# A gated delta-rule layer: from two steps in flight to three, with a new order on every engine

## The chip, the cores and the metric

The kernel runs on one core of one Trainium2 chip. The metric is device time in microseconds, from one launch; lower is better. The engines are TensorE (PE; its weight loads PEld), VectorE (DVE), ScalarE (ACT), GpSimd (POOL) and SyncE (SP), which only issues DMAs. Each runs its own instruction list in order and waits on counting semaphores.

## The reference, cut to what matters

x is 8 x 1024 x 128, float32. The time goes to the attention layer; a small FFN (layer norms, three 128x128 matmuls) follows.

```python
q = silu(causal_conv4(x @ Wq.T)); k = silu(causal_conv4(x @ Wk.T))   # 16 heads of 64
v = silu(causal_conv4(x @ Wv.T))                                     # 16 heads of 128
q, k = q/|q|, k/|k|
alpha = exp(-exp(A_log) * softplus(x @ Wa.T + dt_bias)); beta = 2*sigmoid(x @ Wb.T)
# per batch and head, over t:
S = alpha_t * (S - beta_t * k_t (k_t^T S)) + k_t v_t^T
o_t = S^T q_t
out = rms_norm(o) @ Wo.T
x = x + layernorm(out);  x = x + layernorm(ffn(layernorm(x)))
```

## The kernel before, in words

The recurrence is done in chunks of 64 time points. A step is one chunk of one pair of heads for all 8 batches: 8 head pairs x 16 chunks = 128 steps, in a loop over head pairs and, inside it, chunks. The two heads of a pair lie in partitions 0-63 and 64-127, so most matmuls are 64x64 tiles on the diagonal of the array, 16 or 32 to a phase.

One step, for the names used below:
- proj, tap0, conv (pe_proj, act_tap0 L695, dve_conv L830): four projections j=0..3 (k, q, first and second half of v), each into banks 0-1. ACT writes the first tap, DVE adds three taps. The banks are free for the next projection after its conv.
- silu, norm: ACT applies silu; q and k are squared, summed by a matmul (pe_norm L469), and ACT makes 1/norm by Relu, Ln, Exp. DVE makes KB (normed k, L837), POOL makes qn (L1007).
- decay: POOL makes Lm, three 512-column matmuls (L460) and three Exp (L702) give the decays ex; POOL multiplies them out.
- gram_k, Nd (L478, L845): the matrix N of each 64x64 system. SP writes Nd to scratch, reads back the 16x16 diagonal blocks into NS (scrN, NS). The blocks are inverted by dve_sub in 18 small DVE instructions (L877 to L901). SP writes the inverses (scrZ, scrX), and reads them back as 64x64 tiles (Z, then X in four issues).
- y, z, x, y, z (L541 to L565, L523): two Newton-like doublings from 16 to 64 on PE, with copies by ACT (Y, X, Z) and DVE (Z, L911).
- ks, r, u (L579, L925, L593): k^T S, the right side, the solve; ACT copies U (L763).
- o, ds, s (L610/L614, L624, L932): the output, the update and the new state S = Sg + dS; POOL makes Sg (L1025).
- osq, ms, ln, exp, on, wo, acc: the RMS norm of o (ACT L770, PE L633, ACT L775, L778, DVE L937) and the output projection.

Two steps are in flight. In a loop pass (m, n=m+1) each engine does the solve and output of m between the pieces of the preparation of n. The orders are written out by hand in pe_body, act_body, dve_body, pool_body (through pool_prepare) and sp_body. ScalarE loads its function table twice a pass (L795, L821). SP's order is w_v, wo_s, scrN x2, NS, scrZ, scrX, Z x2, X x4; w_kq is issued by POOL (L983).

Of the kernel before, what the change touches and what calls it, by code (L numbers as in the profile page):

```python
# [79 lines left out]
def build(nc, x, wtab, wo, wab, hcol, cst, wf, mu, out):  # L80
    with ExitStack() as ctx:
# [371 lines left out]
        def pe_decay(pe, n, i):  # L453
            if i < 2:
                if not first(n):
                    pe.wait_ge(r_ok.sem, r_ok.at(n - 1, i + 1))
                pe.wait_ge(lm_ok.sem, lm_ok.at(n, i + 1))
            else:
                pe.wait_ge(dec_ex.sem, dec_ex.at(n, 2))
            nc.tensor.matmul(bank((6, 7, 7)[i]), kc((K_LE, K_GT, K_BD)[i]), half(Lm, min(i, 1)),  # L460
                             start=True, stop=True).then_inc(dec_mm.sem, 1)

        def pe_norm(pe, n, i):
            pe.wait_ge(sqr.sem, sqr.at(n, i + 1))
            if i:
                pe.wait_ge(dec_ex.sem, dec_ex.at(n, 1))
            elif not first(n):
                pe.wait_ge(pt_ok.sem, pt_ok.at(n - 1))
            nc.tensor.matmul(bank((2, 6)[i]), kc(K_BD), half(sq, i), start=True, stop=True).then_inc(nrm_mm.sem, 1)  # L469

        def pe_gram_k(pe, n):
# [3 lines left out]
            for b in range(NB):
                for a, z in HALF:
                    kb = sub_block(BD["KB"], 0, b, a, z)
                    last = nc.tensor.matmul(sub_block(ps, 0, b, a, z), kb, kb, start=True, stop=True)  # L478
            last.then_inc(gram_k.sem, 1)

        def pe_gram_p(pe, n):
            pe.wait_ge(qn_ok.sem, qn_ok.at(n))
# [3 lines left out]
            for b in range(NB):
                for a, z in HALF:
                    last = nc.tensor.matmul(sub_block(ps, 2 * 512, b, a, z), sub_block(BD["KB"], 0, b, a, z),
                                            sub_block(qn, 0, b, a, z), start=True, stop=True)
            last.then_inc(gram_p.sem, 1)  # L490

        def pe_ktr(pe, n):
            pe.wait_ge(kb_ok.sem, kb_ok.at(n))
# [6 lines left out]
            for b in range(NB):  # L500
                for a, z in HALF:
                    last = nc.tensor.matmul(sub_block(ps, 6 * 512, b, a, z), sub_block(BD["KB"], 0, b, a, z),  # L502
                                            k_all[a:z, K_ID + a:K_ID + z], start=True, stop=True)
# [2 lines left out]
        def pe_vtr(pe, n):
            pe.wait_ge(silu_v.sem, silu_v.at(n))
            if not first(n):
                pe.wait_ge(on_ok.sem, on_ok.at(n - 1))
# [4 lines left out]

        def slot(bk, b):
            return ps[:, bk * 512 + (b % 4) * P:bk * 512 + (b % 4 + 1) * P]

        def pe_x(pe, m):
            pe.wait_ge(z_ok.sem, z_ok.at(m, 1))
            pe.sem_inc(pe_go.sem, 1)  # L520
            for b in range(4):
                for a, z in HALF:
                    nc.tensor.matmul(quad(0, b, slice(a, z)), sub_block(BD["Z"], 0, b, a, z),  # L523
                                     k_all[a:z, K_ID + a:K_ID + z], start=True, stop=True)
                for a, z in HALF:
                    last = nc.tensor.matmul(quad(0, b + 4, other(a)), sub_block(BD["Z"], 0, b + 4, a, z),
                                            k_all[a:z, K_ID + a:K_ID + z], start=True, stop=True)
            last.then_inc(x_mm.sem, 1)

        def pe_y(pe, m, l):  # L530
# [8 lines left out]
            for b in range(4):
                for a, z in HALF:  # L540
                    nc.tensor.matmul(quad(l, b, slice(a, z)), sub_block(BD["NM"], 0, b, a, z),  # L541
                                     sub_block(BD["Z"], 0, b, a, z), start=True, stop=True)
                for a, z in HALF:
                    last = nc.tensor.matmul(quad(l, b + 4, other(a)), sub_block(BD["NM"], 0, b + 4, a, z),
                                            sub_block(BD["Z"], 0, b + 4, a, z), start=True, stop=True)
            last.then_inc(y_mm.sem, 1)

        def pe_z(pe, m, n, l):
            if l == 0:
# [9 lines left out]
            xs = BD["X" if l else "X0"]
            for b in range(4):  # L560
                for a, z in HALF:
                    nc.tensor.matmul(quad(1 - l, b, slice(a, z)), sub_block(xs, 0, b, a, z),
                                     sub_block(BD["Y"], 0, b, a, z), start=True, stop=True)
                for a, z in HALF:
                    last = nc.tensor.matmul(quad(1 - l, b + 4, other(a)), sub_block(xs, 0, b + 4, a, z),  # L565
# [777 lines left out]
```

## Time and profile before

| | us |
|---|---|
| median of 3 runs | 4767.3 (4766.52 to 4771.13) |
| profiled execution | 4768.39 |
| its span | 4766.6 |
| mean granted TensorE clock | 0.932 of full |

| engine | busy us | share of the span |
|---|---|---|
| PE | 3981.9 | 84% |
| DVE | 3447.9 | 72% |
| ACT | 2826.5 | 59% |
| POOL | 1620.0 | 34% |

The 128 steps run from about 91 us to about 4560 us; the FFN takes the last 206 us. Before the steps, x is normed and the decay tables are made. A line of the timeline reads: start, duration, engine, line, operation, output and inputs, count; in brackets the idle time before it and who ended it. Starts of consecutive instructions can be closer together than a duration, since they are pipelined.

### The profile page before, as it was taken

To read this page: it belongs to the slowest core of one execution; us is meant where nothing else is said; L and a number is where in the kernel's file an instruction comes from. 1 tells how busy PE (TensorE), PEld (TensorE's weight loads), DVE (VectorE), ACT (ScalarE), POOL (GpSimd) and SP (SyncE) were. 2 spreads that over 40 slices of the span, in tenths; PEclk is the share of its full clock that TensorE was granted. 3 is DMA by queue.
4 is the path that set the end of the run, shared out by engine and by line. 5 is a ranking of instruction groups with operands and counts; after the bars stand their busy time and mean duration, and the time that the engine had idled before them with its cause. 6 is when DMAs were issued, how large, how long until landed. Compare 5 with 4: busy or idle time off the path is not lost. (4 is left out here: it accounts for less than half of the span.)

```text
span 4766.6 us, 171733 instructions
## 1 busy us (share of the span) xinstructions
PE 3981.9 (84%) x67980; PEld 2818.1 (59%) x67980; DVE 3447.9 (72%) x7448; ACT 2826.5 (59%) x4519; POOL 1620.0 (34%) x1574
## 2 busy tenths in 40 slices
PE   5888888888888888888888888888888888888855
PEld 4565665656666565666666565666656566666644
DVE  5777777777777777777777777777777777777745
ACT  2666656666565656656665666656565665666534
POOL 2333333333333333333333333333333333333311
PEclk9999999999999999999999999999999999999977
DMA  1211111121211112121111111121111212111111
GB/s 53 44 38 42 39 38 41 39 43 39 43 38 40 41 37 42 39 43 38 41 40 37 42 39 43 39 42 38 38 43 37 43 39 43 38 41 40 36 39 40
DMA packets 877987, 191.80 MB, mean 40 GB/s; under 512 B 816000, under 2 KB 873600, under 8 KB 877952
## 3 DMA queue, kind: packets, MB, share of 16 engines
q1 hardware_dynamic: 871648, 173.49, 17.3%
q0 software_dynamic: 6304, 17.84, 1.3%
q8 instruction: 22, 0.36, 0.0%
q14 instruction: 13, 0.11, 0.0%
HBM read 136.16 MB, written 55.06 MB: 40 GB/s over the span
## 5 line engine op out<-in xcount | busy, mean ns | idle before, releaser
L830 DVE SCALAR_TENSOR_TENSOR cv<-ps,w_v,cv 128x512 f32<-128x512 f32 x768 | 576.6, 751 | 562.7 <-ACT cv L695 544.6
L830 DVE SCALAR_TENSOR_TENSOR cv<-ps,w_kq,cv 128x512 f32<-128x512 f32 x768 | 575.2, 749 | 139.9 <-ACT cv L695 121.8
L695 ACT ACTIVATE cv<-ps,w_kq 128x512 f32<-128x512 f32 x256 | 175.9, 687 | 623.0 <-PE ps L449 623.0
L502 PE MATMUL ps<-k_all,KB 64*64 64x64 f32 x4096 | 225.4, 289 | 326.3 <-issue 326.3
L460 PE MATMUL ps<-Lm,k_all 128*128 128x512 f32 x768 | 418.5, 626 | 0.0
L997 POOL TENSOR_TENSOR sq<-sl 128x512 f32<-128x512 f32 x128 | 133.0, 1039 | 838.6 <-ACT sl L710 838.6
L990 POOL COPY stP<-tabP 128x24 f32 (+1 forms) x128 | 25.3, 197 | 1144.1 <-DVE KT L859 1144.1
L502 PEld LDWEIGHTS ps<-k_all,KB 64*64 64x64 f32 x4096 | 206.2, 197 | 340.0 <-issue 340.0
L469 PE MATMUL ps<-sq,k_all 128*128 128x512 f32 x512 | 285.1, 639 | 138.6 <-ACT ex L702 138.6
L710 ACT ACTIVATE sl<-cv 128x512 f32<-128x512 f32 x256 | 161.5, 631 | 369.8 <-DVE cv L830 369.8
L449 PE MATMUL ps<-xnT,w_v 128*128 (+1 forms) x1024 | 298.2, 412 | 98.8 <-DVE Nd L845 53.0
L1007 POOL TENSOR_TENSOR qn<-sl,sq 128x512 f32<-128x512 f32 x128 | 162.9, 1272 | 597.2 <-ACT sq L733 597.2
L449 PE MATMUL ps<-xnT,w_kq 128*128 (+1 forms) x1024 | 328.4, 447 | 10.9 <-DMA w_kq<-wtab 7.8
L1025 POOL TENSOR_TENSOR Sg<-S,stR 128x512 f32<-128x512 f32 x256 | 317.4, 1258 | 9.5 <-DVE stR L917 9.5
L775 ACT ACTIVATE oo<-ps,eps 128x512 f32<-128x512 f32 x256 | 175.9, 687 | 238.3 <-PE ps L633 238.3
L883 DVE TENSOR_TENSOR tmpS<-NS,XT 64x8 f32<-64x8 f32 (+5 forms) x768 | 283.4, 369 | 26.4
L925 DVE SCALAR_TENSOR_TENSOR Rr<-ps,stR,Vt 128x128 f32<-128x128 f32 x1024 | 276.4, 342 | 19.4 <-PE ps L579 1.9
L579 PEld LDWEIGHTS ps<-S,KB 64*64 64x64 f32 x4096 | 221.8, 133 | 99.8 <-issue 99.8
L877 DVE TENSOR_SCALAR XT<-NS 64x2 f32<-64x2 f32 x128 | 134.5, 1051 | 194.4 <-DMA NS<-scrN 194.4
L995 POOL TENSOR_TENSOR Lm<-k_all,stP 128x512 f32<-128x512 f32 x256 | 260.9, 1038 | 21.8 <-POOL stP L990 21.6
L449 PEld LDWEIGHTS ps<-xnT,w_v 128*128 128x128 f32 x1024 | 172.6, 188 | 151.1 <-issue 67.1
L610 PEld LDWEIGHTS ps<-QG,S 64*64 64x64 f32 x8192 | 240.6, 135 | 30.5 <-issue 30.5
(184 smaller groups left out, 10890.3 us busy)
## 6 DMA issues: line engine op xcount, KB each, us to landing
scrN<-Nd SPq DMA_DIRECT2D x256, 128.0 KB, 2.4
Z<-scrZ SPq DMA_DIRECT2D x256, 128.0 KB, 2.8
X<-scrX SPq DMA_DIRECT2D x512, 64.0 KB
w_v<-wtab SPq DMA_DIRECT2D x128, 132.0 KB, 2.1
w_kq<-wtab POOLq DMA_DIRECT2D x128, 132.0 KB, 2.4
wo_s<-wo SPq DMA_DIRECT2D x128, 128.0 KB, 2.4
NS<-scrN SPq DMA_DIRECT2D x128, 64.0 KB, 2.5
scrZ<-XT SPq DMA_DIRECT2D x128, 64.0 KB, 2.5
```

The costliest lines, as they stand in the source:

```text
L449: last = nc.tensor.matmul(pj[:, 4 * g:4 * g + 4, 0:CW], w[:, (j % 2) * P:(j % 2 + 1) * P], xnT3[:, 4 * g:4 * g + 4, bass.ds((n % NC) * C, ...
L460: nc.tensor.matmul(bank((6, 7, 7)[i]), kc((K_LE, K_GT, K_BD)[i]), half(Lm, min(i, 1)), start=True, stop=True).then_inc(dec_mm.sem, 1)
L469: nc.tensor.matmul(bank((2, 6)[i]), kc(K_BD), half(sq, i), start=True, stop=True).then_inc(nrm_mm.sem, 1)
L502: last = nc.tensor.matmul(sub_block(ps, 6 * 512, b, a, z), sub_block(BD["KB"], 0, b, a, z), k_all[a:z, K_ID + a:K_ID + z], start=True, sto ...
L579: last = nc.tensor.matmul(slot(6 + g, b)[a:z], sub_block(BD["KB"], 0, b, a, z), unit(S, b)[a:z], start=True, stop=True)
L610: nc.tensor.matmul(o_cols(h, b, d), S[a:z, b * P + d:b * P + d + 64], sub_block(BD["QG"], 0, b, a, z), start=True, stop=False)
L695: nc.scalar.activation(cv4[:, j], pj[:, :, 0:C], ACT.Copy, scale=tap(j, 0)).then_inc(tap0.sem, 1)
L830: nc.vector.scalar_tensor_tensor(cv4[:, j], pj[:, :, k:k + C], tap(j, k), cv4[:, j], ALU.mult, ALU.add).then_inc(conv.sem, 1)
L883: ins = nc.vector.tensor_tensor(t, NB8[:, :, i:i + 1, 0:i].to_broadcast([64, 2, i, i]), XB8[:, :, 0:i, 0:i], ALU.mult)
L925: last = nc.vector.scalar_tensor_tensor(unit(Rr, b), slot(6 + g, b), stR[:, b:b + 1], unit(Vt, b), ALU.mult, ALU.add)
L995: nc.gpsimd.tensor_tensor(v3(Lm, i), over(kc(o, C), NB, C), bcast(stP[:, 0:8], C), ALU.mult).then_inc(lm_ok.sem, 1)
L1025: nc.gpsimd.tensor_tensor(half(Sg, g).rearrange("p (b v) -> p b v", b=4), half(S, g).rearrange("p (b v) -> p b v", b=4), gam, ALU.mult).th ...
```

## The change

Three steps are in flight: a pass is (l, m, n) with m=l+1, n=m+1. Besides:
- Matmuls of 64 rows that used only the two diagonal quadrants of the array are placed by `place(cls, a)`: batches 4 to 7 go to the off-diagonal quadrants. This holds for gram_k, gram_p, ktr, ks, ds and the decays; y, x and z had it already; u keeps two quadrants.
- The decays are one phase of eight 64-row matmuls of 256 columns and one Exp of 1024 columns. The third decay (for QG) comes from a table: it is written once to scrG in DRAM, and SP reads each step's row back, broadcast over 64 partitions, in two DMAs (sp_g).
- The 8x8 triangular inversions move from DVE (13 of dve_sub's 18 instructions) to POOL (pool_elim, 14 instructions); five stay on DVE.
- o waits once for its own earlier matmuls (os_mm).
- w_kq is issued by SP. qg, nm and the mask dmp are done by POOL after qn.

The orders (one pass; `l`, `m`, `n` is the step; conditions left out):

```diff
+ PE:   dec(m) x(l) y(l,1) proj(m,3) gram_k(m) z(l,1) nq(m) u(l) proj(n,0) o(l) ds(l) ms(l)
+       ktr(m) proj(n,1) gram_p(m) ks(m) vtr(m) wo(l) nk(n) proj(n,2) y(m,0) z(m,0)
+ ACT:  tap0(n,0) osq(l,0) osq(l,1) o_ln(l,0) o_exp(l,0) o_ln(l,1) nq_exp(m) o_exp(l,1)
+       TABLE silu_v(m,0) silu_k(n) silu_v(m,1) tap0(n,1) sq_k(n) v(m) silu_q(n) nk_max(n)
+       TABLE tap0(n,2) y(m,0) nk_ln(n) nk_exp(n) exp(n) x(m) y(m,1) tap0(n,3) z1(m)
+       nq_max(n) u(m,0) u(m,1) nq_ln(n)
+ DVE:  conv(m,3)k=2,3 conv(n,0)k=1,2 s(l,0) conv(n,0)k=3 s(l,1) on(l,0) sub(m)0,1 k(m)
+       sub(m)2,3 on(l,1) sub(m)4 p(m) conv(n,1) acc(l) r(m) conv(n,2)k=1 z0(m)
+       conv(n,2)k=2,3 keys(n) str(n) n(n) conv(n,3)k=1
+ POOL: dmp(l) sg(l) qg(l) nm(l) stp(m) lm(m) sq_q(m) dmn(m) elim(m) qn(m)
+ SP:   wkq(n) gram(m) wo(l) wv(n) g(n) inv_out(m) inv_in(m)
```

The waits of the last line, as they stand in the code:

```diff
+        def sp_g(sp, n):
+            if not first(n):
+                sp.wait_ge(qg_ok.sem, qg_ok.at(n - 1))
+            for h, (a, z) in enumerate(HALF):
+                sp.dma_start(half(ex, 2)[a:z], scrG[bass.ds(n, 1), h, :].to_broadcast([C, NB * C])).then_inc(g_in.sem, 16)
...
+        def sp_inv_out(sp, n):
+            sp.wait_ge(sub.sem, sub.at(n, SUBS - 1))
+            sp.dma_start(blocks(scrZ), X16).then_inc(z_out.sem, 16)
+            sp.wait_ge(sub.sem, sub.at(n))
+            sp.dma_start(blocks(scrX), XB[0:64, :].rearrange("g (k j) -> g k j", j=16)).then_inc(x_out.sem, 16)
...
+        def pool_qg(pool, n):
+            pool.wait_ge(qn_ok.sem, qn_ok.at(n))
+            pool.wait_ge(g_in.sem, g_in.at(n))
+            if not first(n):
+                pool.wait_ge(o_mm.sem, o_mm.at(n - 1))
+            nc.gpsimd.tensor_tensor(half(BD["QG"], 0), qn[:], half(ex, 2), ALU.mult).then_inc(qg_ok.sem, 1)
...
+        def pool_elim(pool, n):
...
+            for k in range(7):
+                r, c = 7 - k, k + 1
+                pool.wait_ge(elim.sem, elim.at(n, max(2 * k, 1)))
+                if k == 0:
+                    pool.sem_inc(pool_go.sem, 1)
+                    nc.gpsimd.tensor_copy(XB8[:, :, 0, 1:8], NB8[:, :, 1:8, 0]).then_inc(elim.sem, 1)
+                else:
+                    t = tmpE[0:64, 0:2 * r * c].rearrange("g (u j i) -> g u j i", u=2, j=c)
+                    nc.gpsimd.tensor_tensor(t, NB8[:, :, c:8, k:c].rearrange("g u i o -> g u o i").to_broadcast([64, 2, c, r]),
+                                            XB8[:, :, 0:c, k:c].to_broadcast([64, 2, c, r]), ALU.mult).then_inc(elim.sem, 1)
+                    pool.wait_ge(elim.sem, elim.at(n, 2 * k + 1))
+                    nc.gpsimd.tensor_tensor(XB8[:, :, 0:c, c:8], XB8[:, :, 0:c, c:8], t, ALU.add).then_inc(elim.sem, 1)
...
+        def pe_u(pe, m, n):
+            pe.wait_ge(z_ok.sem, z_ok.at(m))
+            pe.wait_ge(r_ok.sem, r_ok.at(m))
+            if n is not None:
+                pe.wait_ge(dec_ex.sem, dec_ex.at(n))
+                pe.wait_ge(nq_mx.sem, nq_mx.at(n))
```

The other waits that the prediction speaks of: x(l) waits for z0(l); proj(m,3) for conv(m,2); gram_k(m) for keys(m); z(l,1) for x's copy and for n(m), the instruction that writes Nd; y(m,0) for Z in; z(m,0) for X in; ktr(m) for both s(l); nq_exp(m) for its Ln; qn(m) for nq_exp(m); sub(m)0 for elim(m).

## Rows read from the trace of the kernel before

**Rows 1.** The page's first part: busy us, share, instructions of each engine.

```profile
PE 3981.9 (84%) x67980; PEld 2818.1 (59%) x67980; DVE 3447.9 (72%) x7448; ACT 2826.5 (59%) x4519; POOL 1620.0 (34%) x1574
```

**Rows 2.** Waits over the span: us in total, times, longest.

```profile
ACT cv L695 <- PE ps L449: 724.4, 384, 5.6
```

**Rows 3.** Timeline of SP's queue, one step: start, us.

```profile
2409.99 0.57 SPq L1056 DMA_DIRECT2D scrZ<-XT  x1
...
2412.56 1.27 SPq L1063 DMA_DIRECT2D Z<-scrZ  x2
...
2415.87 0.62 SPq L1069 DMA_DIRECT2D X<-scrX  x1
...
2428.44 1.28 SPq L1052 DMA_DIRECT2D scrN<-Nd  x2
2431.55 0.59 SPq L1054 DMA_DIRECT2D NS<-scrN  x1
2444.43 0.57 SPq L1056 DMA_DIRECT2D scrZ<-XT  x1
```

**Rows 4.** Timeline of PE, in the same step.

```profile
2402.89 1.15 PE L488 MATMUL ps<-qn,KB 64*64 64x64 f32 x32
2406.62 1.97 PE L502 MATMUL ps<-k_all,KB 64*64 64x64 f32 x32 [2.58 <-issue]
...
2416.86 0.27 PE L541 MATMUL ps<-Z,NM 64*64 64x64 f32 x2
...
2417.49 1.12 PE L460 MATMUL ps<-Lm,k_all 128*128 128x512 f32 x2
...
2428.56 1.15 PE L449 MATMUL ps<-xnT,w_v 128*128 x4 [0.41 <-DVE Nd L845]
2429.64 1.96 PE L593 MATMUL ps<-Rr,Z 64*64 64x128 f32 x32
...
2435.41 1.98 PE L633 MATMUL ps<-oo,k_all 128*128 128x512 f32 x4
```

**Rows 5.** Granted clock beside L502: us, PE, PEld, DVE, ACT, POOL, PEclk, DMA.

```profile
2406.60:2408.50 1.90, 1.88 (x32) 1.80 (x32) 1.90 (x4) 0.55 (x2) 0.00 (x0) 0.52 0.00 0
```

**Rows 6.** Timeline of ACT, in the same step.

```profile
2431.65 0.60 ACT L763 ACTIVATE U<-ps 128x512 f32<-128x512 f32 x1 [0.28 <-PE ps L593]
...
2433.78 1.08 ACT L770 ACTIVATE oo<-ps 128x512 f32<-128x512 f32 x2 [1.01 <-PE ps L614]
2436.57 0.69 ACT L775 ACTIVATE oo<-ps,eps 128x512 f32<-128x512 f32 x1 [1.70 <-PE ps L633]
...
2438.02 1.14 ACT L778 ACTIVATE oo<-oo 128x512 f32<-128x512 f32 x2
```

**Rows 7.** Timeline of POOL, in the same step.

```profile
2411.67 0.20 POOL L990 COPY stP<-tabP 128x24 f32 x1 [9.05 <-DVE KT L859]
2412.04 2.04 POOL L995 TENSOR_TENSOR Lm<-k_all,stP 128x512 f32<-128x512 f32 x2 [0.17 <-POOL stP L990]
...
2432.85 1.27 POOL L1007 TENSOR_TENSOR qn<-sl,sq 128x512 f32<-128x512 f32 x1 [4.65 <-ACT sq L733]
```

**Rows 8.** Instructions of tile Sg: min/median/max ns, first and last start.

```profile
L1025 POOL TENSOR_TENSOR Sg<-S,stR x2: 1034/1259/1484, 2425.7 to 2427.2; 128x512 f32<-128x512 f32 x2
```

**Rows 9.** Timeline of DVE, in the same step.

```profile
2408.23 1.02 DVE L894 TENSOR_TENSOR tmpS<-XT,tmpW 64x512 f32<-64x512 f32 x1
...
2419.55 1.18 DVE L911 COPY Z<-ps 16x128 f32<-16x128 f32 x4
2422.94 2.32 DVE L830 SCALAR_TENSOR_TENSOR cv<-ps,w_v,cv 128x512 f32<-128x512 f32 x3 [2.21 <-ACT cv L695]
2425.18 1.12 DVE L837 TENSOR_TENSOR KB<-sl,sq 128x512 f32<-128x512 f32 x1
2427.73 0.69 DVE L845 TENSOR_TENSOR Nd<-ps,ex 128x512 f32<-128x512 f32 x1 [1.43 <-PE ps L478]
...
2434.51 0.85 DVE L877 TENSOR_SCALAR XT<-NS 64x2 f32<-64x2 f32 x1 [1.71 <-DMA NS<-scrN]
```

More of the change, by code:

```diff
@@ L33 @@
 NT = T // P
-SUBS = 18
+ELIM = 14
+SUBS = 5
 SK = 16 * C + 16
@@ L451, in pe_proj @@
             last.then_inc(proj.sem, 1)
[L453 to L467, printed above, removed]
-                pe.wait_ge(pt_ok.sem, pt_ok.at(n - 1))
-            nc.tensor.matmul(bank((2, 6)[i]), kc(K_BD), half(sq, i), start=True, stop=True).then_inc(nrm_mm.sem, 1)
+        def pe_dec(pe, n):
+            pe.wait_ge(lm_ok.sem, lm_ok.at(n))
+            if not first(n):
+                pe.wait_ge(r_ok.sem, r_ok.at(n - 1))
+            pe.sem_inc(pe_go.sem, 1)
+            for i, o in enumerate((K_LE, K_GT)):
+                for cls in range(2):
+                    for a, z in HALF:
+                        c = (PAIR_C + cls) * 512 + i * 4 * C
+                        last = nc.tensor.matmul(ps[place(cls, a), c:c + 4 * C], k_all[a:z, o + a:o + z],
+                                                Lm[a:z, i * 512 + cls * 4 * C:i * 512 + (cls + 1) * 4 * C], start=True, stop=True)
+            last.then_inc(dec_mm.sem, 1)
@@ L472, in pe_gram_k @@
             pe.wait_ge(kb_ok.sem, kb_ok.at(n))
-            pe.wait_ge(conv.sem, conv.at(n, 9))
+            if not first(n):
+                pe.wait_ge(x_ok.sem, x_ok.at(n - 1))
             pe.sem_inc(pe_go.sem, 1)
[L475 to L478, printed above, removed]
+            for i in range(4):
+                for cls in range(2):
+                    for a, z in HALF:
+                        kb = blk64(BD["KB"], CLASSES[cls][i], a)
+                        last = nc.tensor.matmul(ps[place(cls, a), col64(PAIR_A, cls, i)], kb, kb, start=True, stop=True)
@@ L483, in pe_gram_p @@
             if not first(n):
-                pe.wait_ge(ms_ln.sem, ms_ln.at(n - 1, 1))
+                pe.wait_ge(ms_ln.sem, ms_ln.at(n - 1))
             pe.sem_inc(pe_go.sem, 1)
[L486 to L489, printed above, removed]
+            for i in range(4):
+                for cls in range(2):
+                    for a, z in HALF:
+                        last = nc.tensor.matmul(ps[place(cls, a), col64(PAIR_A, cls, i)], blk64(BD["KB"], CLASSES[cls][i], a),
+                                                blk64(qn, CLASSES[cls][i], a), start=True, stop=True)
             last.then_inc(gram_p.sem, 1)
@@ L496, in pe_ktr, with pe_vtr @@
             else:
+                pe.wait_ge(nq_mx.sem, nq_mx.at(n))
                 pe.wait_ge(dec_ex.sem, dec_ex.at(n))
-                pe.wait_ge(nrm_mx.sem, nrm_mx.at(n))
             pe.sem_inc(pe_go.sem, 1)
[L500 to L503, printed above, removed]
-            last.then_inc(k_tr.sem, 1)
[L506 to L509, printed above, removed]
+            for i in range(4):
+                for cls in range(2):
+                    for a, z in HALF:
+                        last = nc.tensor.matmul(ps[place(cls, a), col64(PAIR_C, cls, i)], blk64(BD["KB"], CLASSES[cls][i], a),
+                                                k_all[a:z, K_ID + a:K_ID + z], start=True, stop=True)
+            last.then_inc(k_tr.sem, 1)
+        def pe_vtr(pe, m):
+            pe.wait_ge(silu_v.sem, silu_v.at(m))
+            if not first(m):
+                pe.wait_ge(on_ok.sem, on_ok.at(m - 1))
+            else:
+                pe.wait_ge(g_cp.sem, g_cp.at(0))
             for b in range(NB):
@@ L512, in pe_vtr, with pe_y @@
             last.then_inc(v_tr.sem, 1)
[L515 to L530, printed above, removed]
+        def pe_y(pe, m, n, l):
             if l:
-                pe.wait_ge(y_ok.sem, y_ok.at(m, 1))
+                pe.wait_ge(z_ok.sem, z_ok.at(m, 1))
             else:
@@ L535, in pe_y @@
                 pe.wait_ge(nm_ok.sem, nm_ok.at(m))
-                pe.wait_ge(pt_ok.sem, pt_ok.at(m))
-                pe.wait_ge(v_ok.sem, v_ok.at(m))
+                if n is not None:
+                    pe.wait_ge(nk_mx.sem, nk_mx.at(n))
+                if not first(m):
+                    pe.wait_ge(acc_ok.sem, acc_ok.at(m - 1))
             pe.sem_inc(pe_go.sem, 1)
[L539 to L545, printed above, removed]
@@ L557, in pe_z @@
             pe.wait_ge(y_ok.sem, y_ok.at(m, l + 1))
             pe.sem_inc(pe_go.sem, 1)
[L559 to L565, printed above, removed]
-                                            sub_block(BD["Y"], 0, b + 4, a, z), start=True, stop=True)
+            for i in range(4):
+                for cls in range(2):
+                    for a, z in HALF:
+                        b = CLASSES[cls][i]
+                        q = place(cls, a)
+                        last = nc.tensor.matmul(ps[a:z, col64((PAIR_B, PAIR_A)[l], cls, i)],
+                                                BD["X" if l else "X0"][q, b * C:(b + 1) * C],
+                                                BD["Y"][q, b * C:(b + 1) * C], start=True, stop=True)
@@ new lines, in act_u, with act_osq @@
+        def act_u(act, m, g):
+            act.wait_ge(u_mm.sem, u_mm.at(m, g + 1))
+            if first(m):
+                act.wait_ge(g_tr.sem, g_tr.at(0))
+            else:
+                act.wait_ge(ds_mm.sem, ds_mm.at(m - 1))
+            nc.scalar.activation(half(U, g), bank(PAIR_C + g), ACT.Copy).then_inc(u_ok.sem, 1)
+        def act_osq(act, m, h):
+            act.wait_ge(o_mm.sem, o_mm.at(m))
+            if not first(m):
+                act.wait_ge(wo_mm.sem, wo_mm.at(m - 1))
+            nc.scalar.activation(half(oo, h), bank(PAIR_B + h), ACT.Square).then_inc(o_sq.sem, 1)
@@ L1026, in pool_decay_s, with pool_qn @@
                                         gam, ALU.mult).then_inc(sg_ok.sem, 1)
-        def pool_body(pool, m, n):
-            if n is not None:
-                pool_weights(pool, n)
-                pool_prepare(pool, m, n)
-            else:
-                pool_decay_s(pool, m)
+        def pool_qn(pool, n):
+            pool.wait_ge(nq_rn.sem, nq_rn.at(n))
+            if not first(n):
+                pool.wait_ge(gram_p.sem, gram_p.at(n - 1))
+                pool.wait_ge(qg_ok.sem, qg_ok.at(n - 1))
+            nc.gpsimd.tensor_tensor(qn[:], half(sl, 1), sq_qt, ALU.mult).then_inc(qn_ok.sem, 1)
@@ new lines, in sp_inv_in @@
+        def sp_inv_in(sp, n):
+            sp.wait_ge(z_out.sem, z_out.at(n))
+            if not first(n):
+                sp.wait_ge(u_mm.sem, u_mm.at(n - 1))
+            for h, (a, z) in enumerate(HALF):
+                sp.dma_start(v3(BD["Z"], 0)[a:z], rows(scrZ, h)).then_inc(z_in.sem, 16)
+            sp.wait_ge(x_out.sem, x_out.at(n))
+            if not first(n):
+                sp.wait_ge(x_ok.sem, x_ok.at(n - 1))
+            for h, (a, z) in enumerate(HALF):
+                sp.dma_start(v3(BD["X0"], 0)[a:z, 0:4], rows(scrX, h)[:, 0:4]).then_inc(x_in.sem, 16)
+                sp.dma_start(v3(BD["X0"], 0)[other(a), 4:8], rows(scrX, h)[:, 4:8]).then_inc(x_in.sem, 16)
@@ L1097, in _ @@
             def _(pe):
+                for b in range(NB):
+                    last = nc.tensor.transpose(unit(ps, 16 + b), tmp[0][:].rearrange("p (n b) -> p n b", b=NB)[:, :, b], ident)
+                last.then_inc(g_tr.sem, 1)
                 program(pe, pe_body)
```

827 lines of the change are left out of this document (466 added, 361 removed).

## The prediction

> **What bounds the kernel now.** I read the busy shares first [rows 1]: no engine is full. PE, at 84%, comes nearest, and its busy time is flattered, since ends of matmuls are modelled. The waits come next [rows 2]: ACT waits 724.4 us in all for projections, 384 times, so the order of the phases counts more than one engine's load. Then the timeline of one step: scrZ is issued at 2409.99 and again at 2444.43 [rows 3], a period of 34.44 us. 128 such periods are 4408 of the 4766.6 us of the span, so a change of 1 us in the period is worth some 127 us. PE stands idle 2.58 us before L502 [rows 4], and those 32 matmuls then take 1.97 us where the same count and shape takes 1.15 us at L488 [rows 4]; the granted clock beside them is 0.52 [rows 5], the lower of the two levels (1.2 of 2.4 GHz). So a PE gap of that length is paid for a second time.
>
> **What the change removes.** By load alone all is well. 32 matmuls of 64x64 take 1.15 us on two quadrants (L488 [rows 4]), but 0.63 us on four (L541 starts at 2416.86, the next phase at 2417.49). So gram_k, gram_p and ktr cost about 0.6 each, ks and ds about 1.0 instead of 1.96 (the length of L593, the same shape [rows 4]), the three decays 1.0 instead of three times 1.12. That takes 5 to 6 us from PE's 31 (3981.9 over 128 [rows 1]). DVE loses 13 small instructions and gets none. If loads or the compute chain set the period it would be near 30 us. So the question is which cycle of waits closes last, and I walk one pass. Time 0 is the start of u(l); the period T is when u(m) starts.
>
> **Walk, part 1: u(l) to qn(m).** The second U copy starts 2.01 after u and ends at 2.6 (2429.64 to 2431.65, and 0.60 long [rows 4, 6]); proj(n,0), about 1.0 (L449 to L593 is 1.08 [rows 4]), now stands between, so o starts at 2.9. Before, osq started 4.14 after u (2433.78 [rows 6]), that is 2.15 after o; the new self-wait in o must drain the array. I take 0.3, the 0.27 us of one matmul as L541's shows it [rows 4]; bounds 0 and 1.0. osq starts at 5.35, ds runs 5.1 to 6.1, ms starts at 6.1, o_ln 1.16 later (2435.41 to 2436.57 [rows 4, 6]) at 7.3. Then ln, exp, ln, nq_exp follow at about 0.6 to 0.7 each (L775 0.69; two exps in 1.14 [rows 6]): nq_exp ends at 9.7. qn(m) starts at 9.8.
>
> **Part 2: POOL's train.** qn, dmp, sg twice and qg stand in this order: 1.27, 1.27, 2 x 1.03, 1.27 (L1007 [rows 7], the shortest Sg [rows 8]) is 5.8. Beside them DVE does sub(m). DVE and POOL block each other when DVE reads two tensors of SBUF: KB takes 1.12 against 0.69 for Nd, which reads one from PSUM [rows 9], and the Sg that starts beside KB takes 1.48 against 1.03 [rows 8]. sub(m)2, which is L894 with 1.02 us [rows 9], and the copy sub(m)4 (I take 0.4: a 256-column copy) fall inside the train, so POOL loses about 1.4. qg is done at 9.8 + 7.2 = 17.0. Bounds: 15.6 without any blocking, 18.0 if sub(m)0 falls inside too. The Trainium skill, "SBUF — State Buffer", Who interferes with whom, has the same rule: a DVE instruction with two SBUF inputs contends with a GpSimd one that reads SBUF, and the later one fully blocks. The trace agrees here by 0.45 us on Sg. Were it wrong for these forms, T would be 1.4 lower.
>
> **Part 3: SP.** SP's order puts g(n) ahead of inv_out(m), and g(n) waits for qg(m), since it overwrites what qg reads. Behind that waiting DMA stand scrZ, scrX, Z and X of step m. sub(m) itself is done early: DVE reaches it at 9.3 (after s and on), and its five instructions with k and on(l,1) between them end at about 13.7. Its results then lie still until 17.0. The two g issues take 1.28 (as two scrN [rows 3]): scrZ goes at 18.3. From scrZ to Z is 2.57, from Z to the last X 3.31 (2409.99, 2412.56, 2415.87 [rows 3]), and the last X lands some 2.7 later; NS, issued at 2431.55, releases DVE at 2434.51, which is 2.96 [rows 3, 9]. So X of m is there at 26.9 and z(m,0) can start; PE's work ahead of it (ktr, proj, gram_p, ks, vtr, wo, nk, proj(n,2)) was out by about 18.2. PE stands idle about 6 us ahead of y(m,0).
>
> **Part 4: z(m,0) to u(m).** z 0.6, its end to DVE 0.2, z0 1.2 (L911), two convs 1.5 (two of L830's three in 2.32 [rows 9]), proj(n,3) 1.0, gram_k 0.6 and 0.2, Nd 0.7, z(m,1) 0.6, nq 1.1 (as L460 [rows 4]), Relu with its latency 0.9: 8.6. After the idle time PE resumes at the lower clock, as at L502: z takes 1.1 instead of 0.6 and dec 2 instead of 1, which shows only if it outlasts DVE. I add 0.5; bounds 0 and 2.0. The Trainium skill, "TensorE: Matmul & The Clock Gate", Part 1, says that the throttled state is the default and activity releases it. By rows 4 and 5 the step before pays this price once, near L502; by the page it would stand here too, behind the longer gap.
>
> **The sum.** T = 9.8 + 7.2 + 1.3 + 8.6 + 8.6 + 0.5 = 36.0, against 34.44: 1.55 more. 127 periods give 197 us. The ends cost a little: one more pass, and the gain table written and read; I take +5 (bounds -15 and +25). The profiled execution took 4768.39 us, the median of the runs is 4767.3, 1.1 lower, which changes nothing: 4768 + 202 is 4970, rounded to 4965 on the median.
>
> **Costed at nothing, with its cover.** The POOL elimination: Nd is written 2.6 before u, NS lands about 6.1 after that (2428.44 to 2434.51 [rows 3, 9]), so at 3.5. 13 instructions at 0.37 (a tiny POOL copy 0.20 plus 0.17 to the dependent one [rows 7]) end at 8.3, ahead of sub(m)0 at 9.3 and qn at 9.8. Cover 1.0 to 1.5 us; at 0.5 each they end at 10.0, at 0.65 at 12.0, and then T rises by the excess over 9.8. The table loads stand behind o_exp(l,1) and nk_max, and only silu_v, vtr and tap0(n,2) wait for them, all well ahead of 24. The vtr, wo and acc chain has 6 us of slack under the waiting for Z.
>
> **Rivals.**
> 1. *SP's stall hides, the compute chain sets T.* If SP had g out early, y(m,0) would start at about 19 and z at 21.4, and T would be 29.9: 4768 - 4.6 x 127 = 4190. For it: the loads. Against it: the wait on qg(m) is in the code, and qg cannot end before 15.6. Chance 0.06.
> 2. *Same cycle, but shorter (the other side).* POOL's train runs unblocked beside sub (-1.4), the clock costs nothing (-0.5), and the o drain is nil (-0.3): T = 33.8, 4768 - 0.65 x 127 = 4690. It decides in POOL's train: if qg is done earlier than 15.4, the kernel is faster than before, all else as forecast. For it: sub's instructions touch 64 partitions only and the blocked forms in rows 8 and 9 are 128 wide. Chance 0.17.
> 3. *POOL's elimination is slow.* At 0.5 to 0.65 each qn starts at 10.1 to 12.1; T = 36.3 to 38.2, up to 5240. For it: POOL's small instructions here are tensor_tensor with four-dimensional patterns, of which the trace has none. Chance 0.17.
> 4. *PE stays at the lower clock* through x, y, proj and gram_k after the 6 us gap: +1.5 to +2, T about 37.7, 5180. PE is then busy less than two thirds of the time. Chance 0.15.
> 5. The forecast, T 35.3 to 36.8 (4880 to 5070): chance 0.45.
>
> **How the numbers follow.** A difference under 0.2% (10 us) cannot be told from none here. Faster takes rivals 1 and 2 and nothing else: 0.23. Within 0.2% needs T within 0.08 of 34.4: 0.03. Slower: 0.74. The likeliest case gives 4965. The range leaves out rival 1, the better half of the chance below rival 2's value and the tails of 3 and 4: 4690 to 5190. The forecast's own range is 4880 to 5070.
>
> **What would show it.** In the changed trace: SP issues g and then scrZ 1.3 later in every step, both long after sub's last instruction (right: about 4 us after); PE's largest wait is y(m,0) or z(m,0) for the DMA of Z or X, 5 to 8 us a step; qn, dmp, sg, sg, qg stand back to back on POOL, with sg or dmp longer than 1.3; the granted clock is low near y(m,0). Wrong if PE waits less than 3 us for Z and X together, if elim ends after nq_exp, if scrZ is issued straight after sub, or if the period is under 34.

## The result: 7.8% slower, and the profile after

| | before | after |
|---|---|---|
| median us | 4766.95 (4 runs) | 5138.41 (5133.92 to 5141.01, 4 runs) |
| ratio | | 1.0776, 95% interval 1.0757 to 1.0795 |
| profiled execution, its span | 4768.39, 4766.6 | 5137.53, 5135.7 |
| mean granted clock | 0.932 | 0.860 |
| period, mean over the 127 of the trace | 34.67 | 37.50 |

The means are those of the 127 distances from one scrZ issue to the next. The difference of 2.83 us times 127 is 359 of the 369 us by which the span grew.

The first part of the page after, against [rows 1]: PE, DVE and ACT do less, POOL more, and all of PE, DVE and ACT are less full. Nothing is near a load limit.

```profile
PE 3473.2 (68%) x69274; PEld 2478.5 (48%) x69274; DVE 3143.1 (61%) x5785; ACT 2778.7 (54%) x4268; POOL 2070.6 (40%) x3238
```

Its waits (us in all, times, longest). PE's largest for another unit is for Z, which before was next to nothing; POOL waits for nq_exp (L767) with the elimination long done.

```profile
PE ps L584 <- DMA Z<-scrZ: 658.8, 128, 5.6
...
POOL qn L976 <- ACT sq L767: 364.1, 127, 3.6
...
PE ps L614 <- DMA X<-scrX: 98.6, 92, 1.7
```

One pass of SP's queue, against [rows 3]. What is to be seen is the order: ex (that is g), then scrZ, then Z:

```profile
2406.74 0.34 SPq L1024 DMA_DIRECT2D w_v<-wtab  x1
2421.66 1.35 SPq L1035 DMA_DIRECT2D ex<-scrG  x2
2423.16 0.63 SPq L1046 DMA_DIRECT2D scrZ<-XT  x1
...
2426.27 1.27 SPq L1055 DMA_DIRECT2D Z<-scrZ  x2
...
2429.58 0.62 SPq L1061 DMA_DIRECT2D X<-scrX  x1
...
2459.34 1.34 SPq L1035 DMA_DIRECT2D ex<-scrG  x2
```

POOL's train in the same pass, against [rows 7, 8]:

```profile
2411.90 0.22 POOL L1010 TENSOR_TENSOR XT<-XT,tmpE 64x14 f32<-64x14 f32 x1
2414.90 1.27 POOL L976 TENSOR_TENSOR qn<-sl,sq 128x512 f32<-128x512 f32 x1 [2.78 <-ACT sq L767]
2416.14 1.27 POOL L960 TENSOR_TENSOR ex<-ex,k_all 128x512 f32<-128x512 f32 x1
2417.38 2.72 POOL L968 TENSOR_TENSOR Sg<-S,stR 128x512 f32<-128x512 f32 x2
2420.06 1.41 POOL L989 TENSOR_TENSOR QG<-qn,ex 128x512 f32<-128x512 f32 x1
```

DVE beside it, against [rows 9]: L879 is sub(m)2, L882 is sub(m)3, after which scrZ's data are ready.

```profile
2416.28 1.96 DVE L879 TENSOR_TENSOR tmpS<-XT,tmpW 64x512 f32<-64x512 f32 x1
2418.27 0.68 DVE L882 TENSOR_REDUCE XT<-tmpS 64x64 f32<-64x512 f32 x1
```

PE in the same pass, against [rows 4]: u(l), ms, the wait for Z, then y (L584), z (L614), dec (L505) and x (L595), gram_k (L529) and u(m). y, z and x take 1.6 times what gram_k takes at full clock, which is also 32 matmuls of 64x64 on four quadrants (0.69); dec takes 1.99 where it takes 1.09 at full clock (e12 below).

```profile
2404.91 1.96 PE L643 MATMUL ps<-Rr,Z 64*64 64x128 f32 x32 [0.98 <-ACT sq L759]
...
2411.22 1.98 PE L692 MATMUL ps<-oo,k_all 128*128 128x512 f32 x4
...
2429.99 1.13 PE L584 MATMUL ps<-Z,NM 64*64 64x64 f32 x32 [5.19 <-DMA Z<-scrZ]
2432.28 1.13 PE L614 MATMUL ps<-Y,X 64*64 64x64 f32 x32 [1.16 <-DMA X<-scrX]
2433.21 1.99 PE L505 MATMUL ps<-Lm,k_all 64*64 64x256 f32 x16
2434.94 1.11 PE L595 MATMUL ps<-k_all,Z 64*64 64x64 f32 x32
...
2438.19 0.69 PE L529 MATMUL ps<-KB 64*64 64x64 f32 x32
...
2442.58 1.96 PE L643 MATMUL ps<-Rr,Z 64*64 64x128 f32 x32 [0.99 <-ACT sq L759]
```

The granted clock (last but two) from the wait to gram_k, against [rows 5]. It is at the lower level already in the wait and stays there through y, z, dec, x and y(l,1). The third line's 0.78 is the mean of a stretch in which it rose: by that mean it rose at about 2437.4, during proj(n,3), 7.4 us after y began.

```profile
2428.00:2429.90 1.90, 0.00 (x0) 0.00 (x0) 0.00 (x0) 0.00 (x0) 0.00 (x0) 0.50 0.71 160
...
2433.20:2435.00 1.80, 1.80 (x28) 1.10 (x27) 1.46 (x5) 0.00 (x0) 0.00 (x0) 0.50 0.00 0
...
2436.80:2438.10 1.30, 1.30 (x8) 0.88 (x4) 0.95 (x2) 0.60 (x1) 1.26 (x2) 0.78 0.00 0
2438.20:2438.90 0.70, 0.69 (x33) 0.55 (x32) 0.00 (x0) 0.60 (x1) 0.00 (x0) 1.00 0.00 0
```

The whole cycle can be read off these rows. The forecast's 9.1 is its 8.6 and 0.5 together:

| link | forecast | measured | from |
|---|---|---|---|
| u(l) to qn(m) | 9.8 | 9.99 | 2404.91, 2414.90 |
| qn, dmp, sg, qg | 7.2 | 6.57 | 2414.90, 2421.47 |
| qg's end to scrZ | 1.3 | 1.69 | 2423.16 |
| scrZ to z(m,0) | 8.6 | 9.12 | 2432.28 |
| z(m,0) to u(m) | 9.1 | 10.30 | 2442.58 |
| sum | 36.0 | 37.67 | |

### The profile page after: what moved, and what is told of

It reads as the page before. It is cut to its first block and busy times, and to the rows that moved or that the text cites. A ratio compares the mean times of both kernels' runs of the same rounds, so it can differ in the third digit from the quotient of the medians.

```text
span 5135.7 us, 174485 instructions
## 1 busy us (share of the span) xinstructions
PE 3473.2 (68%) x69274; PEld 2478.5 (48%) x69274; DVE 3143.1 (61%) x5785; ACT 2778.7 (54%) x4268; POOL 2070.6 (40%) x3238
## 5 line engine op out<-in xcount | busy, mean ns | idle before, releaser
L584 PE MATMUL ps<-Z,NM 64*64 64x64 f32 x8192 | 284.0, 311 | 658.8 <-DMA Z<-scrZ 658.8
L956 POOL TENSOR_TENSOR ex<-ex,stP 128x512 f32<-128x512 f32 x128 | 175.9, 1374 | 1301.4 <-ACT ex L720 1301.4
L584 PEld LDWEIGHTS ps<-Z,NM 64*64 64x64 f32 x8192 | 252.7, 218 | 709.9 <-issue 709.9
L787 ACT ACTIVATE Y<-ps 128x512 f32<-128x512 f32 x256 | 152.9, 597 | 603.3 <-PE ps L584 603.3
L614 PE MATMUL ps<-Y,X 64*64 64x64 f32 x8192 | 233.9, 270 | 250.7 <-issue 121.9
L643 PE MATMUL ps<-Rr,Z 64*64 64x128 f32 x4096 | 253.1, 272 | 126.4 <-ACT sq L759 125.5
L614 PEld LDWEIGHTS ps<-Y,X 64*64 64x64 f32 x8192 | 199.8, 176 | 284.6 <-issue 284.6
L643 PEld LDWEIGHTS ps<-Rr,Z 64*64 64x64 f32 x4096 | 225.7, 133 | 228.1 <-issue 228.1
L700 PE MATMUL ps<-oo,wo_s 128*128 128x512 f32 x512 | 254.4, 620 | 42.9 <-DVE PT L849 40.4
L921 DVE TENSOR_TENSOR S<-ps,Sg 128x512 f32<-128x512 f32 x256 | 175.6, 687 | 171.3 <-PE ps L685 171.3
```

The costliest lines, as they stand in the source:

```text
L584: last = nc.tensor.matmul(ps[place(cls, a), col64((PAIR_A, PAIR_B)[l], cls, i)], blk64(BD["NM"], b, a), blk64(BD["Z"], b, a), start=True, ...
L614: last = nc.tensor.matmul(ps[a:z, col64((PAIR_B, PAIR_A)[l], cls, i)], BD["X" if l else "X0"][q, b * C:(b + 1) * C], BD["Y"][q, b * C:(b + ...
L643: last = nc.tensor.matmul(ps[a:z, col128(PAIR_C, cls, i)], blk64(BD["Z"], b, a), unit(Rr, b)[a:z], start=True, stop=True)
L700: last = nc.tensor.matmul(bank(3), wo_s[:, h * D:(h + 1) * D], half(oo, h), start=(h == 0), stop=(h == 1))
L787: nc.scalar.activation(two(half(BD["Y"], 0)), pair((PAIR_A, PAIR_B)[l]), ACT.Copy).then_inc(y_ok.sem, 1)
L921: nc.vector.tensor_tensor(half(S, g), bank(PAIR_C + g), half(Sg, g), ALU.add).then_inc(s_ok.sem, 1)
```

## Experiments

All edits are made in the changed kernel (5138 us); e9 adds its edit to that of e1, and e5, e8, e10 and e11 combine edits of order. Ratios are to the kernel before, timed beside them. What was expected stands ahead of each result.

| run | what it does | us | ratio (95%) | mean period |
|---|---|---|---|---|
| e1 | g last in SP's pass | 4492 | 0.943 (0.941-0.945) | 32.43 |
| e2 | qg first on POOL | 4703 | 0.987 (0.986-0.989) | 34.12 |
| e3 | 5 filler matmuls before y | 5045 | 1.059 (1.057-1.061) | 36.78 |
| e4 | 1 us more POOL after elim | 5136 | 1.078 (1.077-1.080) | 37.50 |
| e6 | nq_exp ahead of osq | 4767 | 1.000 (0.999-1.001) | 34.59 |
| e7 | 2 more table loads | 5110 | 1.071 (1.069-1.073) | 37.29 |
| e9 | e1 + 2 more table loads | 4706 | 0.987 (0.985-0.989) | 34.08 |
| e5 | e1 + e2 | 4385 | 0.919 (0.918-0.921) | 31.60 |
| e8 | e5 + sub early | 4378 | 0.918 (0.917-0.920) | 31.58 |
| e10 | e5 + nq_exp early | 4604 | 0.967 (0.964-0.969) | 33.34 |
| e11 | e8 + nq_exp early | 4436 | 0.931 (0.930-0.933) | 32.00 |
| e12 | e3 with 6 + 1 fillers | 5141 | 1.078 (1.077-1.080) | 37.51 |

**e1: SP does g last.**

```diff
                 sp_wv(sp, q)
-                sp_g(sp, q)
             sp_inv_out(sp, n)
             sp_inv_in(sp, n)
+            if q is not None:
+                sp_g(sp, q)
```

> The changed kernel with one edit: SP issues g(n) last in its pass, behind inv_in(m). Theory A (SP stands in g's wait for qg while the finished inverse of step m is queued behind it): scrZ goes out as soon as sub is done, about 14.1 us after u's start instead of 18.3, z(m,0) starts at 22.7 instead of 27.4, PE's idle time ahead of y(m,0) shrinks from 5.2 us to under 1, the clock stays up, and the period falls from 37.68 to 31.5 us: 5138 - 6.2 x 127 = about 4350 us. Rival B (POOL's elimination and train are the load that sets the period, SP only passes it on): period stays above 36, over 4950 us. Rival C (ScalarE's order, two table loads between the silu, sets it): the same, over 4950 us.

646 us went, with every instruction kept. SP's queue and PE in one pass of this run: scrZ at 2406.27 directly follows the end of sub(m)3, g comes after the last X, and PE waits 0.61 for Z; y takes 0.69.

```profile
2406.27 0.58 SPq L1046 DMA_DIRECT2D scrZ<-XT  x1
...
2412.17 0.62 SPq L1061 DMA_DIRECT2D X<-scrX  x1
2412.97 1.22 SPq L1035 DMA_DIRECT2D ex<-scrG  x2
```

```profile
2412.71 0.69 PE L584 MATMUL ps<-Z,NM 64*64 64x64 f32 x32 [0.61 <-DMA Z<-scrZ]
2414.62 0.69 PE L614 MATMUL ps<-Y,X 64*64 64x64 f32 x32 [1.21 <-ACT Y L787]
...
2423.81 1.96 PE L643 MATMUL ps<-Rr,Z 64*64 64x128 f32 x32 [0.99 <-ACT sq L759]
```

Theory A stands; rivals B (POOL's load) and C (ScalarE) fall. The time expected was 142 us too low: I had reckoned with passes of 31.5 alone. 59 of the 127 periods are under 32.0, but 49 are over 32.9, most of them 33.2. In a pass of 33.24 the granted clock is 0.50 from 2472.3 to 2475.6, and wo takes 3.35 where it takes 1.96 in the others:

```profile
2471.82 3.35 PE L700 MATMUL ps<-oo,wo_s 128*128 128x512 f32 x4 [0.33 <-DVE PT L849]
```

wo is that slow (over 2.6 us) in 49 of the 128 passes of e1.

**e2: POOL does qg first.**

```diff
-                pool_dmp(pool, l)
-                pool_sg(pool, l)
                 pool_qg(pool, l)
+                pool_dmp(pool, l)
+                pool_sg(pool, l)
```

> The changed kernel with one edit: POOL does qg ahead of dmp and sg, SP's order as it is. Theory A: qg ends about 11.4 us after u's start, g's wait is over before sub is done, so scrZ again follows sub at about 14.1; period 31.5 to 32.5 us, 4350 to 4480 us, though POOL does as much work as before. Rival B: POOL's load is the same, so no change, 5100 to 5150 us.

435 us went, POOL's work being the same. But the period is 34.1, not 31.5 to 32.5, since g still stood ahead of scrZ: scrZ goes 15.2 us after u (median) instead of 14.1, Z is issued 3.09 after scrZ in the pass read where e1 has 2.59, and PE still waits 2.77 for Z, after which y, z and dec run at the lower clock (1.13, 1.13, 1.99; 9.9 from z to u). POOL and DVE of one pass:

```profile
2412.28 1.28 POOL L976 TENSOR_TENSOR qn<-sl,sq 128x512 f32<-128x512 f32 x1 [2.86 <-ACT sq L767]
2413.79 2.00 POOL L989 TENSOR_TENSOR QG<-qn,ex 128x512 f32<-128x512 f32 x1 [0.24 <-POOL qn L976]
```

```profile
2413.66 1.03 DVE L879 TENSOR_TENSOR tmpS<-XT,tmpW 64x512 f32<-64x512 f32 x1
```

qg must first wait 0.24 for qn's semaphore. In that gap sub(m)2 gets in, runs its bare 1.03 us, and qg takes 2.00. In the changed kernel dmp was there first, and the same sub(m)2 took 1.96. In these two runs whoever comes first makes the other wait.

**e3 and e12: PE kept busy by filler matmuls, whose result nobody reads.**

```diff
                 pe_proj(pe, n, 2)
             if m is not None:
+                pe.wait_ge(v_ok.sem, v_ok.at(m))
+                for k in range(5):
+                    nc.tensor.matmul(bank(PAIR_B), kc(K_BD), k_all[:, 0:512], start=True, stop=True)
                 pe_y(pe, m, n, 0)
```

e12 has 6 in this place, and one more between y(m,0) and z(m,0).

> The changed kernel with five 512-column matmuls (constants, into a bank that is free then, read by nobody) in PE's gap ahead of y(m,0). They give nothing to the computation. If the lower clock after the gap costs 1.2 to 1.7 us of the 10.3 us from z(m,0) to u(m), the granted clock there is 1.0 and the period falls to 36.0 to 36.5 us: 4925 to 4990 us. If the clock costs nothing on the path: no change, 5138 us, or more by what the fillers overrun.

> The changed kernel with six 512-column filler matmuls ahead of y(m,0) and one between y(m,0) and z(m,0), none of which adds to the result. With five fillers alone, dec still took 1.98 us at the lower clock and the time from z to u 9.7 us, against 9.1 forecast. If the short gaps around y are what lets the clock fall there, dec takes 1.1 us, z to u is 8.8, and the period falls from 36.8 to about 36.0: 4950 us. If the clock falls anyway: 5045 us or a little more.

e3 gained 93 us, less than expected: in the pass read y was at full speed (0.69), but dec still took 1.98. e12 missed its expectation. The lower clock did leave y, z and dec (1.09), but it went to wo: four matmuls that take 1.96 in the changed kernel take 3.6 here. PE from z(m,0) to u(m) in e12:

```profile
2434.88 0.69 PE L614 MATMUL ps<-Y,X 64*64 64x64 f32 x32
2435.79 1.09 PE L505 MATMUL ps<-Lm,k_all 64*64 64x256 f32 x16 [0.21 <-issue]
...
2444.16 1.96 PE L643 MATMUL ps<-Rr,Z 64*64 64x128 f32 x32 [0.99 <-ACT sq L759]
```

The granted clock of e12 beside wo and beside z and dec:

```profile
2422.70:2426.20 3.50, 3.46 (x5) 1.51 (x6) 2.06 (x3) 1.41 (x2) 3.42 (x5) 0.52 0.23 72
2433.20:2437.00 3.80, 3.49 (x86) 2.06 (x86) 1.28 (x5) 1.90 (x4) 0.00 (x0) 1.00 0.15 36
```

These two runs give the price of the lower clock between z and u. In e12 z(m,0) starts at 2434.88 and u(m) at 2444.16, 9.28 apart; the median of its passes is 9.2, all at full clock. In e1's pass above it is 9.19. In e3 the clock stays full there in 46 of the 103 passes compared, with 9.2 again. The changed kernel takes 10.3, in the pass read and as its median. So the clock costs 1.1 us a pass on the cycle, some 140 us in all, and e3 got 0.7 of it back.

That e12 takes the same time as the changed kernel is a coincidence: it gains the 1.1 us and loses about as much, because z starts 10.06 after scrZ and not 9.12. wo being late, the six fillers ahead of y, which end at 2433.2, overran Z's arrival.

The gap ahead of vtr and wo is only 1.8 us (vtr waits for on(l,1)). Behind this same gap wo is slow (over 2.6 us) in 124 of 128 passes of e12, in 49 of e1, in 30 of e3 and in 3 of the changed kernel. What decides it is open.

**e4: 1 us more work on POOL.**

```diff
                 pool_elim(pool, m)
+                for k in range(2):
+                    nc.gpsimd.memset(tmpF[:, k * 512:(k + 1) * 512], 0.0)
                 pool_qn(pool, m)
```

> The changed kernel with about 1 us of memsets on POOL between elim(m) and qn(m), into columns nobody reads. Theory A: POOL waits 2.8 us there for nq_exp, so nothing moves: 5138 us within 0.3%. Rival B (POOL's elimination is on the path): 1 us a step, 5265 us.

Nothing moved (5136 us). POOL's wait for nq_exp fell from 2.78 to 1.92 us, so the elimination is covered as the prediction said. A pass of e4:

```profile
2410.52 0.98 POOL L1227 MEMSET tmpF<- 128x512 f32 x2
2413.42 1.27 POOL L977 TENSOR_TENSOR qn<-sl,sq 128x512 f32<-128x512 f32 x1 [1.92 <-ACT sq L768]
```

**e6: ScalarE does nq_exp(m) first.**

```diff
+            if m is not None:
+                act_nq_exp(act, m)
             if l is not None:
                 act_osq(act, l, 0)
                 act_osq(act, l, 1)
                 act_o_ln(act, l, 0)
                 act_o_exp(act, l, 0)
                 act_o_ln(act, l, 1)
-            if m is not None:
-                act_nq_exp(act, m)
-            if l is not None:
                 act_o_exp(act, l, 1)
```

> The changed kernel with one edit: ScalarE does nq_exp(m) ahead of osq(l), where it sits idle 1.8 us, and not behind three of the norm's instructions. Theory A (the period is the cycle u, qn, POOL's train, g, scrZ, X, z, u): qn starts when elim is done, 2.7 us earlier, and the whole cycle shortens by that: period 34.8, about 4795 us, though no engine does less. Rival C (ScalarE's load or its table loads set the period): no change, 5138 us.

2.9 us a pass, 372 us in all, from moving one instruction of 0.62 us: the first link of the cycle is real, and this alone brings the changed kernel level with the one before.

**e7 and e9: two more table loads.**

```diff
             act.preload_act_table_set("silu_and_others")
+            act.preload_act_table_set("natural_log_exp_and_others")
+            act.preload_act_table_set("silu_and_others")
             if m is not None:
                 act_silu_v(act, m, 0)
```

> The changed kernel with two more table loads (2.57 us of ScalarE) in every pass, ahead of silu_v(m). Theory A: they lie under PE's 5 us of waiting for Z, so 5138 us within 0.5%. Rival C: 2.57 us a pass, 5460 us; half of it, 5300 us, if vtr carries it on.

> The same two added loads in the kernel with g last (4492 us), where PE waits only 0.6 us for Z. Theory A: the cover is gone, vtr starts 1.3 us later and with it wo, nk, proj(n,2) and y; the period rises by 0.7 to 1.3 us, 4580 to 4660 us. If the loads cost nothing here too: 4492 us.

In the changed kernel 2.57 us more of loading costs nothing; it is even 28 us faster, just outside the 0.5% expected. PE waits 3.34 instead of 5.19 for Z in the pass read, the mean granted clock is 0.879 instead of 0.860, and z to u takes 10.0 (median) instead of 10.3; that the clock alone makes the 28 us is likely but not shown. With g last the same loads cost 1.65 us a pass, 214 us, more than expected. vtr's gap grows from 1.80 to 3.06 and is now for ScalarE's silu:

```profile
2420.78 1.09 PE L566 MATMUL ps<-k_all,sv 128*128 128x128 f32 x8 [3.06 <-ACT sv L743]
...
2428.63 1.51 PE L505 MATMUL ps<-Lm,k_all 64*64 64x256 f32 x16
2429.89 1.13 PE L595 MATMUL ps<-k_all,Z 64*64 64x64 f32 x32
```

1.26 is the delay. The rest goes with the clock, whose mean is 0.914 where e1 has 0.957: in this pass dec and x are slow (1.51 for 1.09, 1.13 for 0.69), in the next one vtr (1.97 for 1.06).

**e5, e8, e10, e11: orders combined.** e5 has the edits of e1 and e2, e10 those and the edit of e6. e8 is e5 with this edit of DVE's order, and e11 has all four:

```diff
                 dve_s(dve, l, 1)
-                dve_on(dve, l, 0)
             if m is not None:
-                dve_sub(dve, m, 0, 2)
+                dve_sub(dve, m, 0, 4)
+            if l is not None:
+                dve_on(dve, l, 0)
+            if m is not None:
                 dve_k(dve, m)
-                dve_sub(dve, m, 2, 4)
```

> The changed kernel with g last in SP's pass and qg first in POOL's. Theory A: once SP no longer waits for qg, an earlier qg brings only what it changes for sub: sub(m)2 gets the shared port first (1.03 us as in the run with qg first, and not 1.96) and scrZ goes 0.9 us earlier, of which 0.6 at most is wanted by y(m,0): 4410 to 4480 us. If the two gains were separate, they would add: 4492 - 435 = 4060 us.

> g last, qg first, and DVE does sub(m)0 to 3 right behind s(l), with on(l,0) and k(m) after them. Theory A: scrZ goes 1.5 to 2 us earlier, but PE reaches y(m,0) only 0.4 us after it can today and z waits for ScalarE's copy and for X; the cycle is then set by PE's and ScalarE's own order, and little is left: 4320 to 4385 us. If scrZ still set it, 1.5 us a pass: 4195 us.

> g last, qg first, nq_exp(m) ahead of osq(l). In the changed kernel that edit brought 2.9 us a pass. Theory A: with g out of the way qn is off the cycle, so it brings next to nothing: 4340 to 4385 us. If it were POOL's load that counts: another 2.9 us, 4015 us.

> All four edits of order: g last, qg first, sub early, nq_exp early. Theory A: no better than the best of the parts by more than 0.5 us a pass: 4280 to 4370 us.

e5 is 107 us faster than e1, the better of its parts, and far from the sum (4060); it is a little faster than the range expected. e8 is faster by 7 us, within the intervals of the ratios: in e5, z waits 1.46 for X and PE reaches y only 0.4 us before Z, so an earlier scrZ is not wanted. Both beat the kernel before by 8%. e10 was a miss: the edit that brought 372 us in e6 costs 219 us here. The trace of e10, POOL and DVE:

```profile
2420.85 1.27 POOL L989 TENSOR_TENSOR QG<-qn,ex 128x512 f32<-128x512 f32 x1 [0.24 <-POOL qn L976]
2422.08 1.72 POOL L960 TENSOR_TENSOR ex<-ex,k_all 128x512 f32<-128x512 f32 x1
```

```profile
2421.78 0.89 DVE L872 TENSOR_TENSOR tmpS<-NS,XT 64x512 f32<-64x512 f32 x1
...
2423.90 1.72 DVE L879 TENSOR_TENSOR tmpS<-XT,tmpW 64x512 f32<-64x512 f32 x1
```

POOL's train now lies on sub(m)0 as well; L872 and L879 together lose 0.9 us (0.67 and 1.03 unhindered), and scrZ goes 14.0 us after u where it goes 13.1 after u in e5. on(l,1) behind them is late, PE has two gaps (0.78 ahead of ks, where e5 has none, and 1.85 ahead of vtr, where e5 has 0.87), and the clock falls: vtr takes 1.94 for 1.06, wo 2.44 for 1.96.

```profile
2424.12 1.10 PE L628 MATMUL ps<-S,KB 64*64 64x128 f32 x32 [0.78 <-DVE KT L856]
2427.07 1.94 PE L566 MATMUL ps<-k_all,sv 128*128 128x128 f32 x8 [1.85 <-DVE oo L925]
2428.81 2.44 PE L700 MATMUL ps<-oo,wo_s 128*128 128x512 f32 x4
```

e11 missed too: 4436 us lies 66 us above its range and 58 above e8, from which it differs by the early nq_exp alone. So with g last that move cost time in both orders tried, in e5's and in e8's. In the pass read ks waits 2.06 for k(m), and the mean granted clock is 0.915 where e8 has 0.945. How the 58 us are made up is open.

```profile
2435.98 1.10 PE L628 MATMUL ps<-S,KB 64*64 64x128 f32 x32 [2.06 <-DVE KT L856]
```

## Why the prediction was right, and where its sizes were off

The forecast was 4965 us, 4% slower; measured is 5138, 7.8% slower. That lies in the range given (4690 to 5190) and above the forecast's own range (4880 to 5070), and the period read, 37.67, lies above its 35.3 to 36.8. The cycle was right; most of its links were sized too small.

**The cycle.** Right, shown from three sides: taking g out of the way (e1), shortening what leads to g at POOL (e2) and at ScalarE (e6). The signs named in the forecast are in the trace: scrZ goes 1.50 after g and 4.2 after sub(m)3 has ended, PE's largest wait is the 5.19 for Z, the two sg take 1.36 each, and the clock is low near y(m,0). Rival 1's condition, g out early, is what e1 made: 32.4 us a pass and not 29.9. In e1's pass z starts 22.4 after u and not 21.4 (PE's own order, with 1.8 us of waiting ahead of vtr and 1.21 for ScalarE's copy of Y), z to u takes 9.2 and not 8.5, and in 49 passes wo is slow. That the reduced loads are worth something only once the stall is gone is what e1 and e5 show.

**Part 1** (9.8, measured 9.99). Right. The drain in o was taken at 0.3; the trace has a wait of 0.18 there.

**Part 2** (7.2, measured 6.57). The blocking is there, but I charged POOL with all of sub(m)2. sub(m)2 came 0.14 us after dmp had begun, so DVE lost 0.9 (L879 takes 1.96 for 1.03), and POOL lost 0.66 at sg (2.72 for 2 x 1.03) and 0.14 at qg. The loss on DVE was free, for scrZ stood behind g. This error of 0.6 hid part of the others: with the train sized rightly the forecast would have been lower still. Rival 2 needed 5.8 here (the four lengths add to 5.87) and the clock at no cost; it had neither.

**Part 3** (1.3 + 8.6, measured 1.69 + 9.12). Right in kind, 0.9 too small: scrZ to Z takes 3.11 against the 2.57 of [rows 3]; in e1, with g behind, it is 2.59. So about 0.5 us goes with the two 128 KB transfers issued just ahead of a small one that is waited for. The median of the changed kernel is 3.03, that of e1 2.59.

**Part 4** (9.1, measured 10.30). The largest miss, and two terms share it. The 8.6 at full clock should have been 9.2, as e1 and e12 show. The shortfall is spread over the links: in e1's pass proj(n,3) comes 3.70 after z and not 3.5, gram_k 4.81 and not 4.5, z(l,1) 6.46 and not 6.0, u 9.19 and not 8.6. The step "I add 0.5" for the clock should have been 1.1. I had the lower clock show in z, and in dec only if it outlasts DVE. But x and y(l,1) ran at it too, and they hold up proj(n,3), which starts 4.55 after z in the changed kernel and 3.70 in e1, and then takes 1.43 for 1.17. In the step of [rows 4, 5] the lower clock had lasted 3.5 us (0.51 from 2406.6 to 2410.1, then 1.00); here it lasted until 7.4 us after y began. Rival 4 named this. Its period of 37.7 is nearly the one measured, but by chance: it adds 1.5 to 2.0 to the 0.5, and the clock cost 1.1 in all. The rest of the 1.67 between forecast and measured period comes from Part 3, from the 8.6 and from Part 1, less what Part 2 had too much.

**The base.** I multiplied the difference from one period of 34.44 us. The mean is 34.67, since periods before run from 34.1 to 35.5. The difference in means is 2.83 against the forecast 1.55; on the means the forecast would have been 1.33. The ends cost about 10 where I took 5.

**Costed at nothing.** POOL's elimination: the 12 instructions behind its first copy take 0.21 to 0.26 and come 0.33 apart, where I took 0.37; it ended 2.78 us before qn, and e4 showed the cover. The table loads: e7 showed them covered; e9 that with the stall gone they are not. Rival 3 did not occur.

## What to carry to other kernels

An in-order DMA queue is an engine with an order of its own. When a change adds an issue with a wait, list what is queued behind it and who needs that soonest; here one prefetch that nobody needed for a whole pass held back the inverse that PE was waiting for, and moving three lines turned 7.8% slower into 5.7% faster. Price a link on the cycle it lies on: the same one-instruction move was worth 372 us in one order and cost 219 us in another. Read the period as a mean over many steps before multiplying by their number.

## What was not expected of the hardware

The granted clock fell in the 5.2 us gap ahead of y(m,0) and stayed at 0.50 until 7.4 us after y began. Behind y only z has a gap (1.16); from z on PE worked without one, and the clock still came back only 5.1 us later. Behind the 2.58 us gap of [rows 4, 5], also followed by work without gaps, it was back after 3.5 us. Why it stayed low for longer here is open. With filler matmuls in the gap the low phase did not vanish but turned up elsewhere (wo at 0.52 in e12), behind a gap of 1.8 us that is followed by a slow wo in 124 of 128 passes there, in 49 in e1 and in 3 in the changed kernel. Two-input DVE instructions on 64 partitions are blocked by POOL as those on 128 are (1.96 for 1.03, 0.89 for 0.67), and block it (2.00 for 1.27).
